# First layer's conditioning product: x as the moving operand over eight 64x32 tiles of TensorE's array, turned by VectorE, issued between the second and third column group

## The reference

```python
def _L0_cond_ref(x, weights, condition):        # weights (16, 64, 64)
    W = weights[condition]                      # one 64x64 matrix for each batch
    return jnp.einsum('bct,bcd->bdt', x, W)     # (128, 64, 1024)

# _L0_ffn_ref, on y = _L0_cond_ref(...), rows of 1024:
    out = y @ W_base.T + b_base + 2 * (experts' rank-16 products, top 2 of 8 by a router on y)
# first layer
    x = x + _L0_ffn_ref(_L0_cond_ref(x, L0_cond_weights, itok_B_0_15), ...)
```

## Time and profile before

| | |
|---|---|
| median of 3 runs | 2044.39 us (2043.88 to 2045.46) |
| the profiled execution's own time | 2044.62 us |
| its span, first to last instruction | 2042.8 us |
| phase 1 | up to about 1041 us of the span |
| TensorE busy | 2017.2 us, 99% |
| VectorE busy | 1410.8 us, 69% |
| ScalarE, GpSimd busy | 394.0 us, 518.9 us |

### The profile page before, as it was taken

One profiled execution on the slowest core, in us unless ns is written; L12 is line 12 of the kernel. 1 busy time (PEld: TensorE's weight loads), 2 busy tenths in 40 slices (PEclk: granted clock), 3 DMA queues, 4 the chain that ended last, 5 costly groups with the idle time before them and its releaser, 6 DMA issues.

```text
span 2042.8 us, 36073 instructions
## 1 busy us (share of the span) xinstructions
PE 2017.2 (99%) x12032; PEld 1890.9 (93%) x12032; DVE 1410.8 (69%) x3754; ACT 394.0 (19%) x1084; POOL 518.9 (25%) x470
## 2 busy tenths in 40 slices
PE   6999999999999999999999999999999999999998
PEld 6999999999999999999988888888888888888887
DVE  6787766666655555555557777777777777777777
ACT  3121111111111111111121122112112112211211
POOL 3665311111111111111122223223223222222322
PEclk8999999999999999999999999999999999999999
DMA  7854433344333333333355655665666666566564
GB/s 238 246 172 148 132 108 102 103 122 115 100 95 103 107 104 94 94 109 105 103 165 162 158 159 153 170 162 150 172 159 157 164 164 160 153 172 162 147 173 113
DMA packets 220201, 289.92 MB, mean 142 GB/s; under 512 B 97795, under 2 KB 169477, under 8 KB 220166
## 3 DMA queue, kind: packets, MB, share of 16 engines
q1 hardware_dynamic: 220166, 289.56, 51.2%
HBM read 163.62 MB, written 109.05 MB: 133 GB/s over the span
## 4 chain that ended last, share of the span: by engine, by line
PE 97%; DVE 2%; SPq 1%; DMA 0%; issue 0%; ACT 0%; DVEq 0%; ACTq 0%
PE bank_g L946 13%; PE bank_g L948 13%; PE bank_g L947 13%; PE bank_g L1000 12%; PE bank_g L999 12%; PE bank_g L998 12%; PE bank_f L1008 10%; PE bank_t L929 5%; PE bank_g L973 1%; PE bank_g L974 1%; PE bank_g L975 1%; PE bank_g L1043 1%; SPq L359 0%; DVE st_l L863 0%; DMA wq<-b 0%
## 5 line engine op out<-in xcount | busy, mean ns | idle before, releaser
L946 PE MATMUL bank_g<-w0h,st_h 128*128 128x384 f32 (+1 forms) x1536 | 522.3, 340 | 3.0 <-DVE w0l L727 2.9
L948 PE MATMUL bank_g<-w0h,st_l 128*128 128x384 f32 (+1 forms) x1536 | 521.3, 339 | 0.0
L947 PE MATMUL bank_g<-w0l,st_h 128*128 128x384 f32 (+1 forms) x1536 | 521.0, 339 | 0.0
L998 PE MATMUL bank_g<-w1h,st_h 128*128 128x352 f32 x1536 | 505.7, 329 | 3.8 <-DVE st_l L863 3.8
L1000 PE MATMUL bank_g<-w1h,st_l 128*128 128x352 f32 x1536 | 496.5, 323 | 0.0
L999 PE MATMUL bank_g<-w1l,st_h 128*128 128x352 f32 x1536 | 495.7, 323 | 0.0
L863 DVE TENSOR_TENSOR st_l<-xbuf,st_h 128x512 fp32r<-128x512 f32 x128 | 212.5, 1701 | 189.3 <-ACT st_h L669 189.3
L548 POOL TENSOR_TENSOR xbuf<-xbuf,b_base_sb 128x1024 f32<-128x1024 f32 x64 | 153.9, 2405 | 697.3 <-PE bank_t L929 683.9
L998 PEld LDWEIGHTS bank_g<-w1h,st_h 128*128 128x128 f32 x1536 | 289.1, 188 | 12.5 <-DVE st_l L863 4.4
L946 PEld LDWEIGHTS bank_g<-w0h,st_h 128*128 128x128 f32 x1536 | 289.7, 189 | 3.9 <-DVE w0l L727 3.9
L999 PEld LDWEIGHTS bank_g<-w1l,st_h 128*128 128x128 f32 x1536 | 289.1, 188 | 1.5
(11 more groups left out here) (79 smaller groups left out, 2078.3 us busy)
## 6 DMA issues: line engine op xcount, KB each, us to landing
xbuf<-x SPq DMA_DIRECT2D x64, 512.0 KB, 4.1
x_scratch<-x1buf SPq DMA_DIRECT2D x64, 512.0 KB, 2.9
x1t_scratch<-x_blocks SPq DMA_DIRECT2D x256, 128.0 KB, 2.3
xbuf<-x1t_scratch SPq DMA_DIRECT2D x64, 512.0 KB, 3.7
x1buf<-x_scratch SPq DMA_DIRECT2D x64, 512.0 KB, 5.2
out<-obuf SPq DMA_DIRECT2D x64, 512.0 KB, 2.7
b_stack<-b_split SPq DMA_DIRECT2D x384, 64.0 KB, 3.7
raw<-a_split SPq DMA_DIRECT2D x128, 128.0 KB, 4.3
```

The source lines that it names most:

```text
L946: pe.matmul(to, st_h[:, rows], w0h[:, k, cols], start=(k == 0), stop=False)
L947: pe.matmul(to, st_h[:, rows], w0l[:, k, cols], start=False, stop=False)
L948: last = pe.matmul(to, st_l[:, rows], w0h[:, k, cols], start=False, stop=(k == KC - 1))
L998: pe.matmul(to, st_h[:, rows], w1h_k[:, k, cols], start=(k == 0), stop=False)
```

## The change

The product is written the other way round. x is the moving operand and the weights are stationary: `wpair` holds the two 64x64 matrices of a tile one below the other (128 partitions x 64 columns), with no zero blocks, so the memset and its semaphore go. A matmul takes one batch's 64 rows (j), 32 of its 64 output columns (s) and a quarter of x, 256 columns (q). Its place in the array is one of eight 64x32 tiles, row half j and column quarter q. Sixteen such matmuls make the product, and its result is laid out unlike the old one: quarter q of the long axis on partitions 32q to 32q+31, in `bank_y`, which is the phase 2 bank `bank_f` under another name. VectorE turns it with two 32x32 block transposes of 128x512 into `bank_t` (`turn_y`), which raise st_ps now. The blocks of the contraction come out in another order, for which the host permutes the rows of the weights `m0`. The product is issued after group 1 instead of after group 2. Since the turned rows are then ready while group 2 still reads `st_h`, ScalarE's `st_hi` also waits for st_used, raised by group 2 at its fourth and eighth block. GpSimd's bias waits for y_ps instead of st_ps[1]. The waits for x and its weights stand ahead of the eighth block of group 1.

```diff
-            wbd = sb("wbd", [P, 2, P], F32, p1)
+            wpair = sb("wpair", [P, 2, CH], F32, p1)
...
-                sp.wait_ge(wbd_zeroed, 1)
...
-                        sp.dma_start(wbd[rows, b, rows],
+                        sp.dma_start(wpair[rows, b, :],
                                      wc[bass.ds(which, 1)].rearrange("a c d -> (a c) d")).then_inc(wc_loaded[b], 16)
...
-                pool.memset(wbd[:, :, :], 0.0).then_inc(wbd_zeroed, 1)
...
-                    pool.wait_ge(st_ps[1], t + 1)
+                    pool.wait_ge(y_ps, t + 1)
...
-                def st_hi(t):
+                def st_hi(t, used):
                     for h in range(2):
                         act.wait_ge(st_ps[h], t + 1)
+                        if used is not None:
+                            act.wait_ge(st_used[h], used)
...
+                def turn_y(t):
+                    dve.wait_ge(y_ps, t + 1)
+                    blocks = bank_y[:, :, :].rearrange("p j (s k i) -> p k (j s) i", s=2, k=KC)
+                    for h in range(2):
+                        ks = slice(h * KC // 2, (h + 1) * KC // 2)
+                        dve.transpose(bank_t[:, h, :].rearrange("p (k g i) -> p k g i", k=KC // 2, g=4),
+                                      blocks[:, ks]).then_inc(st_ps[h], 1)
...
                     move_hw(dve.tensor_copy, 1)
                     if more:
+                        turn_y(n)
+                    if more:
                         st_lo(n, 0)
...
+                def cond(b):
+                    for s in range(2):
+                        cols = slice(s * D // 4, (s + 1) * D // 4)
+                        for q in range(4):
+                            for j in range(PER_TILE):
+                                rows = slice(j * CH, (j + 1) * CH)
+                                last = pe.matmul(bank_y[32 * q:32 * q + 32, j, cols],
+                                                 wpair[rows, b, 32 * s:32 * s + 32],
+                                                 xbuf[rows, b, q * D // 4:(q + 1) * D // 4],
+                                                 start=True, stop=True)
+                    last.then_inc(y_ps, 1)
...
+                        if loads is not None and k == KC - 1:
+                            cond_in(b, loads, n)
...
+                        if g == 2 and k % (KC // 2) == KC // 2 - 1:
+                            last.then_inc(st_used[k // (KC // 2)], 1)
...
-                    if more:
-                        cond(n, 1 - b, loads)
+                        if g == 1 and more:
+                            cond(1 - b)
...
         "m0": lay(np.concatenate([np.asarray(L0_ffn_A).reshape(ER, D), np.asarray(L0_ffn_W_router),
-                                  np.asarray(L0_ffn_W_base)]).T),
+                                  np.asarray(L0_ffn_W_base)]).T
+                  .reshape(4, KC, D // (4 * KC), W0_COLS).transpose(1, 0, 2, 3).reshape(D, W0_COLS)),
```

More of the change, by code:

```diff
@@ L97, in build @@
         bank_f = whole.enter_context(nc.psum_tensor("bank_f", [P, 2, 512], F32))
+        bank_y = bank_f
         w1h = sb("w1h", [P, KC * W1_COLS], F32R)
@@ L170, in build @@
             b_base_loaded = sem("b_base_loaded")
-            wbd_zeroed = sem("wbd_zeroed")
+            y_ps = sem("y_ps")
             st_ps = [sem(f"st_ps{h}") for h in range(2)]
+            st_used = [sem(f"st_used{h}") for h in range(2)]
             hi_done = [sem(f"hi_done{h}") for h in range(2)]
@@ L630, in _ @@
                     if n == 1:
-                        st_hi(0)
+                        st_hi(0, None)
                 def tile(t, more):
@@ L641, in tile @@
                     if more:
-                        st_hi(t + 1)
+                        st_hi(t + 1, t + 1)
                 def scale_weight(u):
@@ L666, in turned_hi @@
                     act.wait_ge(turned_loaded[b], 16 * loads)
-                    act.wait_ge(main_done, t + 1)
+                    if isinstance(t, int) and t == 0:
+                        act.wait_ge(st_used[1], TILES)
+                    else:
+                        act.wait_ge(main_done, t)
                     for h in range(2):
@@ L728, in _ @@
                     if n == 1:
+                        turn_y(0)
                         st_lo(0, 0)
@@ L921, in _, with cond_in, bank @@
             def _(pe):
-                def cond(t, b, loads):
+                def cond_in(b, loads, turned):
                     pe.wait_ge(x_loaded[b], 16 * loads)
                     pe.wait_ge(wc_loaded[b], 32 * loads)
[L927 to L934, removed]
+                    if turned is not None:
+                        pe.wait_ge(st_ps[1], turned)
+                def cond(b):
[9 more added lines that the diff above has]
+                    last.then_inc(y_ps, 1)
+                def bank(g, n, split=True, loads=None, b=None):
                     cols = slice(G0_START[g], G0_START[g] + G0_WIDTH[g])
@@ L958, in tile @@
                             pe.wait_ge(x1_done[g], t)
-                        last = bank(g, n, prior)
+                        last = bank(g, n, prior, *((loads, 1 - b) if g == 1 and more else ()))
                         if g == 0:
                             last.then_inc(h_ps, 1)
-                        if g == 2 and not more:
-                            last.then_inc(main_done, 1)
-                    if more:
-                        cond(n, 1 - b, loads)
+                        if g == 1 and more:
+                            cond(1 - b)
                     for e in range(2):
@@ L976, in tile @@
                           .then_inc(acc_ps[g], 1)
-                cond(0, 0, 1)
+                cond_in(0, 1, None)
+                cond(0)
                 tile(0, 0, 1, False, True)
```

## The result

The changed kernel took 2020.58 us in the median of four runs (2019.35 to 2025.72), against 2044.93 us for the kernel before on the same chips: ratio 0.9884, 95% interval 0.9873 to 0.9896. It is 24 us, 1.2%, faster. I had forecast 2186 us, slower, with a range of 1995 to 2208. The sign is wrong; that the time lies in the range is no merit, since the range had been drawn over cases of both signs. What came is rival 1, all eight tiles at once.

What follows compares the result with a forecast made beforehand. TensorE, busy 2017.2 of 2042.8 us, was taken as the bound: 2044.62 us, plus 140 for 62 products at +2.26 us each, plus 1 for the start, gave 2186 us, slower; range 1995 to 2208.

Steps and rivals of the forecast that it cites:

- rival 1: In the product, all eight tiles work at once in both passes: 1.19 us a product, kernel 2013 us, faster; chance 0.35.
- The bound: Whole kernel: TensorE's list sets the time, busy 2017.2 of 2042.8 us; changes to its length count in full.
- the price of a pass: In the new product, one of 32 passes of 256 columns takes 0.214 us.
- the order argument: In the product, a second pass waiting for its tile holds up everything behind it in the list; 3.64 us a product.
- 17 pass times: In the product, each matmul moves the list on by one pass, one more at the end: 17 x 0.214 = 3.64 us.
- The change of shape: Around each product, full array to tiles and back costs 0.33 us, bounds 0 and 0.66.
- rival 4: Second weights land 1 us late in every tile: TensorE waits 25 us, 2038 us on top of rival 1; chance 0.05.
- the cover of 0.6 us: Second weights land at 906.2, due at 906.8 in group 1's eighth block; at the median it costs nothing.
- VectorE's transposes: Two transposes of the product's result, 1.42 us a tile, costed at nothing.
- my 2 us chain: Behind the product, turn, copy and subtract would cost about 0.71 + 0.60 + 0.69 = 2 us without cover.
- the x1 additions, none due before group 2 ends: In VectorE's list, the x1 additions queued behind its wait for the product are not due before group 2 ends; costed at nothing.
- Tile 0: Tile 0's product hides in its 6.18 us stall; the first product takes up to 7.3 us; 1 us charged.

Runs made afterwards that it cites:

- e8: Changed kernel with eight more matmuls ahead of each product, all on one tile of the array: 2222.6 us, ratio 1.0864 to the kernel before.
- e7: Changed kernel with the sixteen matmuls of each product issued twice in a row: 2070.8 us, ratio 1.0123 to the kernel before.
- e1: Changed kernel with the product's matmuls reordered so that four passes in a row ask for one tile: 2023.9 us, ratio 0.9896 to the kernel before.
- e11: Changed kernel with the product in two halves, the second in the middle of group 2, one more change of shape: 2043.75 us, ratio 0.9991.
- e2: Changed kernel with the tiles' product put back behind group 2: 2094.1 us, ratio 1.0238 to the kernel before.
- e5: Changed kernel with 64x64 weight loads issued first in SyncE's tile and GpSimd's third piece served behind the tile's own DMAs: 2021.6 us, ratio 0.9879.
- e10: Changed kernel with two GpSimd pieces a tile instead of three and the 64x64 weight loads issued first in SyncE's tile: 2017.4 us, ratio 0.9869.
- e12: e10 with GpSimd starting its pieces only after VectorE's moves into hwt, in every tile that has pieces: 2018.3 us, ratio 0.9866.
- e13: e10 with GpSimd starting its pieces only after VectorE's moves into hwt, in tile 0 alone: 2015.5 us, ratio 0.9852.

## Why the prediction was wrong

- **The bound and the price of a pass were right.** TensorE's list sets the time. A pass of 256 columns costs 0.216 us (forecast 0.214): the sixteen starts on one tile in e8 are 0.218 us apart, and four more bunches cost 0.87 us in e7.
- **The step that failed is the order argument**: "the second pass of one tile waits for its first, and everything behind it waits as well". It took the order of starts in a trace in which every matmul uses the whole array, where nothing could overtake, for a rule about tiles. e1 and e8 show passes overtaking up to three waiting ones of another tile, so the forecast's 17 pass times, 3.64 us, are 4, about 0.86 us. Passes of other matmuls between the two of one were the sign that I had named against the argument. The Trainium skill's sentence (TensorE: Matmul & The Clock Gate, Part 3), that matmuls start in program order, does not hold here: e8's seven passes at 952.95 start before one listed ahead of them. Its other statement, that small tiles work concurrently, does hold. "Two records of one matmul never let another's in between" was all that I had against rival 1, and it came from the same rows, in which nothing could have got in between; by my own words they did not forbid the rival. They decided nothing, and yet the forecast's sign hung on them.
- **The change of shape** was charged 0.33 us a product. In the steady period a product took 1.79 us before (1.71, and 0.08 because the second matmul behind it came late); the period fell by 0.56, so it takes 1.23 now. Less the body of 0.86 that leaves 0.37, as e11 measured. Right in size. What fills the time is open (see e11).
- **Rival 1 gave 2013 us, and 2020.6 came.** The steady gain is 0.56 a tile (rival: 0.52), 34 us over 61 periods; the first tiles gave 9 of it back (6.5 in waits, the rest with them and in the clock), which puts the sum at 25 us where the spans differ by 25.3.
- **The loads were rival 4's subject**, with the wrong place: not every tile 1 us late, but tiles 3 to 6 alone, 9 us in all. I had read the cover of 0.6 us in a quiet tile at 900 us and costed it at nothing. In the first 14 tiles SyncE also serves GpSimd, and in tiles 2 to 5 of the changed kernel the cover was gone. (The cover before was 5.3 us, 911.52 less 906.2, not the 4.8 that I wrote; nothing hangs on it.)
- **VectorE's transposes** (1.31 us, forecast 1.42) are hidden, as said; without their cover (e2) they cost more than my 2 us chain suggested, since the x1 addition is queued behind them. That was the sentence "the x1 additions, none due before group 2 ends", true only in this place.
- **Tile 0** absorbed its two products, as forecast, though for less than I had put there: from the first product to group 0 it took 4.86 us instead of 3.46, where the forecast had up to 7.3 for the product alone. The matmul that ends the stall for hwt starts at 35.73 (36.92 before).

## What to carry to other kernels

A row in which two things never could have overlapped is no evidence that they cannot; a rule read off it must not carry the forecast's sign. Small fp32 matmuls paid here on tiles of the array even with two passes each: 32 passes in four pass times, with up to three passes waiting for one tile, for about 0.37 us of changing shape there and back. So change shape once. Moving a step forward in one list shortens the cover of its loads, and that is to be checked in the busiest tiles, at the start, not in a quiet one.

## What the runs showed of the hardware that was not expected

- Passes of matmuls on free tiles started ahead of up to three waiting passes of another tile (e1, e8); with more than three waiting, the free tiles stayed idle (e8, from 949.89 to 952.95).
- The eight starts of a bunch filled 0.05 us in the change, and about twice that in e1, where three passes of the same tile lie between neighbours.
- Across the change between full array and tiles no weight load was taken ahead of its matmul (885.46 and 886.49), and there and back cost 0.36 to 0.37 us (e11).
- After a wait of 3.03 us TensorE was granted 0.50 of its clock for about 3 us; after waits of 0.9 and 1.7 us it was not slowed (the changed kernel).
- VectorE's twelve 32x64 fp32r copies took 2.38 us alone and 6.39 to 7.84 us beside GpSimd's elementwise instructions (e5, e10), and 2.38 us again when GpSimd was made to wait (e12, e13). The Trainium skill (SBUF — State Buffer, SBUF: two separate sides) states that VectorE, in some of its instructions, and GpSimd share one port pair, and that whichever instruction begins first holds it to its end. The trace agrees: in e10 a single copy lasted up to 2.28 us instead of 0.18, in the time of a GpSimd addition of 2.33 us (34.75 to 37.08), while ScalarE's four copies into the same buffer took 1.05 us in e10 as in e13.
